# Two attentions in parts of 256 queries, with maxima two units ahead and the first part's chain inside the second

## The reference, cut to what matters

```
# layer 2, causal
Q, K, V = relu(x@Wq+bq), relu(ctx@Wk+bk), relu(ctx@Wv+bv)
o = softmax(where(tril & (sum(K) != 0), Q K^T / 4, NEG)) V
x = x + relu(o @ Wo + bo);   x = (x - mean) / (std_ddof1 + 1e-8)
# layer 3
sa = mha(x, x, mask: 0 <= i-j < 64, bias: slope_h * (j - i))       # banded
x  = layernorm(x + sa) * g1 + be1
ca = mha(x, ctx, no mask)                                          # cross, "FULL"
x  = layernorm(x + ca) * g2 + be2
x  = layernorm(x + gelu(x @ w1 + b1) @ w2 + b2) * g3 + be3         # w1: 256 x 1024
```

## Time and profile before

| | |
|---|---|
| median of 3 runs (lowest to highest) | 1594.84 us (1594.17 to 1596.35) |
| the profiled execution / its span | 1590.74 / 1588.9 us |
| granted TensorE clock, mean | 0.965 |
| PE, PEld busy | 1426.6 us (90%), 713.9 (45%) |
| DVE, ACT, POOL busy | 864.6 (54%), 716.6 (45%), 263.6 (17%) |

### The profile page before, as it was taken

One profiled execution on the slowest core, in us unless ns is written; L12 is line 12 of the kernel. 1 busy time (PEld: TensorE's weight loads), 2 busy tenths in 40 slices (PEclk: granted clock), 3 DMA queues, 4 the chain that ended last, 5 costly groups with the idle time before them and its releaser, 6 DMA issues.

```text
span 1588.9 us, 23992 instructions
## 1 busy us (share of the span) xinstructions
PE 1426.6 (90%) x8204; PEld 713.9 (45%) x8232; DVE 864.6 (54%) x2099; ACT 716.6 (45%) x1177; POOL 263.6 (17%) x138
## 2 busy tenths in 40 slices
PE   5999898888999988888999998988899998988886
PEld 2336555423533654543443464553263355455334
DVE  2663565585266256567355536556636635655762
ACT  0663353455366234427446425352825632625462
POOL 1004131301100413220110213121011041303001
PEclk9999999989999989998999998998999999999898
DMA  9000404303200230540310031242031005043210
GB/s 339 22 1 12 102 1 91 70 14 113 68 1 7 38 70 1 99 75 1 126 55 1 8 62 45 38 86 51 1 127 54 1 8 106 2 71 64 41 60 14
DMA packets 44776, 85.28 MB, mean 54 GB/s; under 512 B 10464, under 2 KB 27872, under 8 KB 44384
## 3 DMA queue, kind: packets, MB, share of 16 engines
q1 hardware_dynamic: 41136, 73.17, 18.6%
q10 hardware_dynamic: 3504, 10.39, 3.2%
HBM read 43.68 MB, written 2.10 MB: 29 GB/s over the span
## 4 chain that ended last, share of the span: by engine, by line
PE 62%; DVE 15%; issue 10%; ACT 5%; SPq 3%; DMA 3%; ACTq 1%; POOL 0%; DVEq 0%; POOLq 0%
PE ring L1286 8%; PE obank L1296 8%; PE ring L1276 7%; DVE nmax L1075 7%; PE ring L1463 6%; PE ring L1252 6%; PE ring L1352 4%; PE ring L1603 3%; PE obank L1513 3%; PE ring L1201 3%; ACT q_all L771 3%; PE ring L1454 2%; SPq L413 2%; DVE rbuf L1094 2%; DMA q_all<-q_parts 1%
## 5 line engine op out<-in xcount | busy, mean ns | idle before, releaser
L1075 DVE TENSOR_REDUCE nmax<-ring 128x2 f32<-128x1024 f32 (+1 forms) x192 | 218.5, 1175 | 51.3 <-PE ring L1463 33.7
L679 ACT ACTIVATE region_e<-region_d,nmin 128x512 f32<-128x512 f32 x256 | 182.6, 714 | 83.7 <-DVE nmin L936 82.6
L936 DVE CUSTOM_DVE_ANT_0 region_d<-ring,maskb 128x512 f32<-128x512 f32 x256 | 165.9, 686 | 91.5 <-issue 89.4
L784 ACT ACTIVATE region_e<-ring 128x1024 f32<-128x1024 f32 x192 | 183.4, 992 | 55.7 <-PE ring L1463 32.7
L771 ACT ACTIVATE q_all<-ring 2x1024 fp32r<-2x1024 bf16 x96 | 97.6, 1016 | 204.7 <-PE ring L1524 204.2
L606 POOL TENSOR_TENSOR nat_x<-nat_n,rows 128x1024 f32<-128x1024 f32 x16 | 37.6, 2353 | 606.1 <-DVE nat_n L985 461.2
L1286 PE MATMUL ring<-region_q 64*128 64x512 f32 x512 | 126.9, 615 | 6.7 <-ACT region_q L668 5.4
L1454 PE MATMUL ring<-cbf 64*128 64x128 bf16 (+2 forms) x1280 | 131.7, 286 | 0.0
L1071 DVE TENSOR_REDUCE nmax<-ring 128x4 f32<-128x512 f32 (+1 forms) x96 | 86.1, 911 | 75.0 <-PE ring L1454 74.3
L1296 PE MATMUL obank<-region_e,vs 128*64 128x512 f32 x512 | 124.0, 605 | 0.0
L780 ACT ACTIVATE region_e<-ring 128x768 f32<-128x768 f32 (+1 forms) x96 | 74.0, 776 | 55.1 <-PE ring L1454 52.8
(11 more groups left out here) (193 smaller groups left out, 2171.4 us busy)
## 6 DMA issues: line engine op xcount, KB each, us to landing
q_all<-q_parts SPq DMA_DIRECT2D x192, 64.0 KB, 2.5
region_e<-in_w_f SPq DMA_DIRECT2D x8, 1024.0 KB, 5.8
k_tiles_a<-k_parts SPq DMA_DIRECT2D x96, 64.0 KB, 2.3
k_tiles_b<-k_parts SPq DMA_DIRECT2D x96, 64.0 KB, 2.3
q_all<-q_parts ACTq DMA_DIRECT2D x96, 64.0 KB, 3.2
wvo<-in_wv SPq DMA_DIRECT2D x5, 1024.0 KB, 5.1
wqk<-in_wq SPq DMA_DIRECT2D x4, 1024.0 KB, 9.1
wqk<-in_wk SPq DMA_DIRECT2D x4, 1024.0 KB, 11.1
```

The source lines that it names most:

```text
L679: ins = act.activation(e0[:, n % E0, h, :], sm0[:, n % 2, h, :], ACT.Exp, bias=nmin0[:, n, h:h + 1], scale=-1.0, accum_out=sum0[:, n, h:h ...
L784: act.activation(e16[:, n % 4, 2 * u:2 * u + 2, 0:nq], slot((a, "B", g, kt, u))[:, :, 0:nq], ACT.Exp)\
L936: ins = dve.tensor_tensor_reduce(out=sm0[:, n % 2, h, :], in0=slot(("S0", p, kt))[:, h, :], in1=maskb[:, :], scale=-1.0, scalar=3.0e38, op ...
L1075: dve.tensor_reduce(nmax[:, qt, 2 * u:2 * u + 2], slot(name)[:, :, 0:nk], AX.X, ALU.max, negate=True)\
```

## The change

Causal and cross attention are cut into two parts h of 256 queries (`HALVES`), and their *units* are (h, g), eight instead of four. A causal part sees only its own keys: the first part two tiles, the second four. Pass B takes all four heads of a unit for 256 queries in one job. Banded attention keeps one part, but all three now use one order, `attention_steps`:

```diff
+def attention_steps(a):
+    all_units = units(a)
+    first, second = maxima_of(a, 0), maxima_of(a, 1)
+    half = len(second) // 2
+    steps = first + [("M",) + all_units[0]] + second[:half] + [("T",) + all_units[0]] + second[half:] + [("M",) + all_units[1]]
+    waiting = []
+    for n, (h, g) in enumerate(all_units):
+        ahead, keys = maxima_of(a, n + 2), key_tiles(a, h)
+        for i, kt in enumerate(keys):
+            steps.append(("B", h, g, kt))
+            waiting.append(("V", h, g, kt))
+            if len(waiting) > 2:
+                done = waiting.pop(0)
+                steps.append(done)
+                if done[3] == key_tiles(a, done[1])[-1]:
+                    steps.append(("H",) + done[1:3])
+            steps += ahead[len(ahead) * i // len(keys):len(ahead) * (i + 1) // len(keys)]
+            if i == 0 and n + 1 < len(all_units):
+                steps.append(("T",) + all_units[n + 1])
+            steps += CHAINS.get((a, n, i), [])
+        if ahead:
+            steps.append(("M",) + all_units[n + 2])
+    return steps + waiting + [("H",) + all_units[-1]]
+CHAINS = {
+    (CAUSAL, 5, 0): [("O", 0)],
+    (CAUSAL, 5, 1): [("NV", 0)],
+    (CAUSAL, 5, 3): [("NR", 0), ("NN", 0)],
+    (CAUSAL, 6, 1): [("X", 0)],
+    (CAUSAL, 6, 3): [("KS", 0)],
+    (CAUSAL, 7, 0): [("KL", 0)],
+    (CAUSAL, 7, 1): [("QS", 0)],
+    (CAUSAL, 7, 2): [("QL", 0)],
+    (FULL, 5, 0): [("O", 0)],
+    (FULL, 5, 1): [("NV", 0)],
+    (FULL, 5, 3): [("NR", 0), ("NN", 0)],
+    (FULL, 6, 1): [("X", 0)],
+}
...
-    jobs += attention_jobs(CAUSAL) + [("O2", j) for j in range(2)] + [("VC", j) for j in range(2)] + [("X", 2), ("KS",), ("QS",)] + [("VS", j) for j in range(2)] + [("KC",)]
+    jobs += attention_jobs(CAUSAL) + [("VC", 0), ("O2", 1), ("VC", 1), ("VS", 0), ("X", 2, 1), ("KS", 1), ("QS", 1), ("VS", 1), ("KC",)]
...
-    jobs += attention_jobs(FULL) + [("OC", j) for j in range(2)] + [("V0", 2), ("X", 4)]
-    jobs += [("F1", j) for j in range(FT // 2)] + [("F2", j) for j in range(2)]
+    jobs += attention_jobs(FULL) + [("F1", 0, 0), ("OC", 1), ("F1", 0, 1), ("X", 4, 1), ("V0", 2), ("F2", 0), ("F1", 1, 0), ("F1", 1, 1), ("F2", 1)]
...
-        e16 = region_e[:, :].rearrange("p (u s q) -> p u s q", u=4, s=4)
+        e16 = region_e[:, 0:4096].rearrange("p (u s q) -> p u s q", u=4, s=4)
...
-                            if kind == "B":
-                                if which == [0, 2 if a == CAUSAL else 3, 0]:
-                                    for k in range(1, GROUPS):
-                                        act.wait_ge(k_stacked[k], (b * 3 + a + 1) * 96)
-                                exponentials(a, *which)
...
+                rsqrt(3, 1, -1)
+                act.wait_ge(pv_done, (b + 1) * PV_ITER)
+                gelu(0, 0)
+                drain_half_x(4, 1)
+                gelu(0, 1)
+                for j in range(2):
+                    gelu(1, j)
...
+                def drain_half_out(a, h):
+                    part, name = slice(2 * h, 2 * h + 2), (OUT_JOB[a], h)
+                    dve.wait_ge(*filled_by(name, b))
+                    dve.tensor_tensor(nat_y[:, part, :], slot(name)[:, :, 0:D], (nat_y if a == CAUSAL else nat_x)[:, part, :], ALU.add)\
+                        .then_inc(*ends_drain(name))
+                    dve.wait_ge(*drained_by(name, b))
+                    if a == CAUSAL:
+                        link(dve.scalar_tensor_tensor(out=nat_y[:, part, :], in0=nat_y[:, part, :], scalar=0.0, in1=nat_x[:, part, :],
+                                                      op0=ALU.max, op1=ALU.add))
+                    link(moments(h))
+                    variances(NORM_OF[a], h)
```

661 lines of the change are left out of this document (372 added, 289 removed).

## The result

| | before | changed |
|---|---|---|
| median of 4 runs (lowest to highest) | 1595.59 us (1594.17 to 1599.4) | 1678.61 us (1667.3 to 1680.64) |
| span of the profiled execution, mean granted clock | 1588.9 us, 0.965 | 1678.8 us, 0.933 |

A forecast was written before the change was run, and what follows sets the result against it. TensorE was taken to bound causal attention and the last stage, no engine full in cross attention; +4.9 us per batch plus 0.6 for lumps, times four 22, on 1590.7 gave 1612.7, as median 1617; 8-in-10 range 1580 to 1642.

The forecast's parts named there:

- the price of units 6 and 7 of causal attention: Causal attention's last two units, without maxima: scores and values 9.7 us plus moved X, KS, QS halves, 12.6 in all.
- the price of M in banded attention: The two maxima columns cost 0.5 us with their link, taken as no less at half width, eight for four.
- the clock: Half clock returning was left to a rival, at +8 us per batch; the forecast sum had no term for it.
- Causal attention, +11.0 forecast: Causal attention, summed unit by unit by the slower engine, ends at 629.1 against 618.1: 11.0 us longer per batch.
- Unit 5: Causal attention: 7.0 us plus 5.2 for O, NV and NN, 12.2, with a gap of about 3 before pass B.
- The chain, -6.6: Chain behind causal attention: first banded scores 20.0 us after the last values, against 26.6; 6.6 saved per batch.
- the end, -1.4: From cross attention's last values to the next batch: 36.6 us against 38.0, 1.4 saved per batch.
- Banded attention, -0.3: Starts 4.4 us late, ends 4.1 late, so gives back 0.3, despite TensorE standing about 3 for late third-group strips.
- Cross attention, +2.2: Cross attention: earlier opening, VectorE-bound units of 7.0 us, end of 9.9; 65.6 against 63.4 in all.
- B: Rival: half clock returns in about half the units VectorE bounds, +8 us per batch, 1649 us; chance 0.13.
- A: Rival: TensorE stays the bound, the ring evens out and waits vanish, -6.9 us per batch, 1567 us; chance 0.15.
- C: Rival: no difference; openings' 4.6 and 4.3 us return whole, unit 5's stall half as long, about 1595; chance 0.10.

The follow-up runs named there:

- overlap_slots: Changed kernel with norm_late's and gpsimd_late's edits, and GpSimd's four causal instructions each in a gap between VectorE's small operations: 1629.9 us, ratio 1.0222.
- behind_slots: chains_behind with third_late's and gpsimd_late's edits, and GpSimd's four causal instructions each in a gap between VectorE's small operations: 1597.2 us, ratio 1.001.
- third_late: Changed kernel, with banded attention's third head group's maxima starting behind the first group's third pass B instead of its first: 1678.9 us, ratio 1.0522.
- lead_only: Kernel before, whole parts of 512 queries, only the order changed: maxima two head groups ahead, T one ahead, in all attentions: 1658.9 us, ratio 1.0377.
- gpsimd_late: Changed kernel, with GpSimd's cross-key split and second preset in banded attention waiting for the fourth group's maxima columns: 1651.5 us, ratio 1.0347.
- warm_in_t: Changed kernel with three extra matmuls of 512 columns ahead of each T's wait for its maxima: 1665.9 us, ratio 1.0422.
- norm_late: Changed kernel, causal and cross attention: first part's sum one pass B earlier, its normalization behind the last maxima columns: 1653.6 us, ratio 1.0334.
- chains_behind: Changed kernel with both parts' projections, sums, normalizations, turnings and layers behind the attentions, none inside: 1615.7 us, ratio 1.0118.

## Why the prediction was right in direction and wrong in size

**Where the forecast failed.** Three steps of it: the price of units 6 and 7 of causal attention, the price of M in banded attention, and the clock, which its sum left as it was. The chains and the end were priced right.

**Where the 83 us are.** overlap_slots is 34.6 us over the kernel before, behind_slots 1.9. So 49 us of the 83 went with four mends, and the half clock that they took along: GpSimd's instructions out of the way of VectorE's, in banded and in causal attention, and a sum and a normalization in another place on VectorE. Some 33 us are left with the overlap, though the two kernels differ in third_late as well, which may be up to 5 of them. Clock is part of these too: the middle of the runs' mean clocks is 0.956 in overlap_slots and 0.966 in behind_slots, by which at most some 17 us of the 33 are ungranted clock (an estimate: 0.044 of 1630 us less 0.034 of 1597). The profiled executions, of which overlap_slots' is its fastest, differ by 22 us. The halves and the two units of lead together, with their stalls mended, cost next to nothing; neither was judged alone, since lead_only's 61 us have GpSimd's holds in them.

**Causal attention, +11.0 forecast, +18.3 measured, +11.9 in overlap_slots.** In the third batch of the changed kernel, by the first pass B of each unit, against the forecast:

| | first pass B | units 0, 1 | 2, 3 | 4 | 5 | 6, 7 |
|---|---|---|---|---|---|---|
| forecast | 5.3 | 9.5 | 12.8 | 7.0 | 12.2 | 12.6 |
| changed | 4.9 | 6.8 | 13.2 | 10.8 | 13.6 | 18.9 |
| overlap_slots | 5.4 | 6.8 | 13.4 | 8.2 | 10.8 | 14.8 |
| behind_slots | 4.9 | 6.8 | 12.3 | 8.4 | 7.0 | 10.4 |

Units 2 and 3 were forecast well, the first two 2.6 us too long, which by luck hides that much of the misses behind them, and unit 4 too short: its "7.0" is 8.0 in the second batch and 10.8 to 11.0 in the others, where 7 us of half clock lie in it or at its edge. The largest step that failed is "units 6 and 7 ... 12.6 with the last wait". Its own terms, 9.7 and 0.65 + 1.75 + 1.75, add up to 13.9, so the 12.6 was a slip; measured they are 10.4 and 0.91 + 2.00 + 2.00, 15.3. At full clock both units take 15.8 in the second batch, and 14.8 in overlap_slots, where the wait at T is shorter; the 18.9 of the other three batches has 3 us of half clock in it. So the moved work was priced 1.3 us too low by the slip and 1.4 by its terms, and the clock at nothing. Unit 5 was right: 12.0 to 13.6 for 12.2, and the wait of 2.31 us for the sum behind O is the gap of "about 3 us" that was named.

**The chain, -6.6 and -6.2, and the end, -1.4 and -2.7**, were right in the main; the end came out 1.3 us per batch better. The first banded scores come 20.4 us after the last values; 20.0 was said.

**Banded attention, -0.3 and +5.2.** The wait of "about 3 us" for the third group is there, 2.71 in the second batch. What failed is the price of M: "0.5 with their link" from the earlier trace rows holds only where GpSimd stands still. The fourth group's M took 2.3 us in every batch, T waited 2.4, and the clock of the stage, between 0.91 and 1.00 before, is between 0.82 and 0.88. gpsimd_late takes 4.0 of the 5.2 away.

**Cross attention, +2.2 and +6.8, +3.1 in overlap_slots.** Units 1 to 4 take 28.8 for 28.0, unit 5 11.2 for 11.1. Units 6 and 7 take 11.9 to 14.5 for 9.9: without the turning they are 10.8 in behind_slots, which the forecast put too low, and 11.7 in overlap_slots; 14.4 and 14.5 stand in the two batches with the most half clock in these units.

**The rivals.** B was given 0.13 and is a large part of the truth: half clock came back in causal units 2 to 6, in banded attention and at the end of cross attention, and part of it, in units 2 to 4, in just the units that VectorE bounds, where B had put it. The measured 1678.6 lies beyond B's 1649, since the stalls come on top. From the mean clocks, 0.067 of 1678.8 us against 0.035 of 1588.9 were not granted, 112 against 56 us. So at most some 57 of the 83 us are clock, and warm_in_t gave back 13 net of its own matmuls. I held it against B that the steady part of cross attention stood at 0.98. It still does, at 0.99, with waits of 0.4 to 0.9 us in each unit:

```profile
751.00:757.00 6.00, 5.16 (x28) 2.77 (x30) 3.96 (x6) 3.96 (x5) 0.00 (x0) 0.50 0.72 263
757.00:795.00 38.00, 30.34 (x296) 14.69 (x292) 31.71 (x54) 24.93 (x29) 0.00 (x0) 0.99 0.00 1
795.00:811.30 16.30, 14.32 (x148) 6.56 (x148) 6.70 (x20) 12.06 (x16) 0.00 (x0) 0.90 0.01 2
```

But that did not carry over to causal attention. There half clock stands behind waits of 0.65 and 1.01 us and, in norm_late, behind 0.86 and 0.56, while four waits of 2.08 us there and one of 1.83 in the changed kernel were not followed by it. Most of the stalls of 1.4 to 2.5 us inside the changed kernel's attentions were. So long stalls and short waits both precede it, and which wait brings it these runs do not settle; what the forecast had wrong is that it priced every wait at its own length. The Trainium skill ("TensorE: Matmul & The Clock Gate", A second HAM failure mode) tells of a kernel in which short idles between groups of matmuls let the clock fall again and again; causal attention agrees with that, and the 38 us above do not. A is refuted: even with every stall mended causal attention takes 60 us. C is refuted for the changed kernel. Its time is that of behind_slots, but not its mechanism: there nothing overlaps, so no stall of unit 5 was halved.

**Why the overlap does not pay.** The moved work is TensorE's and stands in units where TensorE is the bound (6, 7), so it cannot cost less than its length; and O, X and the projections go through the ring of three slots that the scores need. That these slots cost something beyond the length was not tested by itself. In behind_slots against overlap_slots causal attention gives 9.4 for a chain of 5.3, cross attention 3.1 for 1.7 at the end. TensorE's idle time in units 2 and 3, where the chain would have been free, comes before the first part is finished. That the overlap costs more than it saves is shown, in chains_behind against the changed kernel and again with the stalls mended; how its cost divides into length, ring and clock is in part argued.
